# Three scatter accumulators instead of two in an attention and mixture-of-experts block

## The reference, cut to what matters

```
x = x + attention(layernorm(x), ctx)
xn2 = layernorm(x)
scores = softmax(xn2 @ gate_w.T);  topk_w, topk_i = top_k(scores, 4)   # T = 1024 tokens
buf[e]  = tokens of expert e, at most CAP = 128, the rest filled with the spare row T
eout[e] = (silu(xpad[buf[e]] @ w_gate[e]) * (xpad[buf[e]] @ w_up[e])) @ w_down[e] * wbuf[e]
y       = zeros.at[buf].add(eout)[:T]                 # scatter-add over all experts
out     = x + y + silu(xn2 @ sw_gate) * (xn2 @ sw_up) @ sw_down
```

## Time and profile before

| what | value |
| --- | --- |
| median of three timed runs | 219.53 us (214.23, 219.53, 221.49) |
| the profiled execution's own time | 214.88 us |
| its span | 213.1 us, so 1.78 us lie around it |
| PE busy | 185.3 us (87%) |
| DVE busy | 128.1 us (60%) |
| Pool busy | 96.3 us (45%) |
| granted TensorE clock, mean | 0.984 |

### The profile page before, as it was taken

One profiled execution on the slowest core, in us unless ns is written; L12 is line 12 of the kernel. 1 busy time (PEld: TensorE's weight loads), 2 busy tenths in 40 slices (PEclk: granted clock), 3 DMA queues, 4 the chain that ended last, 5 costly groups with the idle time before them and its releaser, 6 DMA issues.

```text
span 213.1 us, 3899 instructions
## 1 busy us (share of the span) xinstructions
PE 185.3 (87%) x1369; PEld 137.5 (65%) x1369; DVE 128.1 (60%) x360; ACT 80.8 (38%) x173; POOL 96.3 (45%) x128
## 2 busy tenths in 40 slices
PE   7884785889798999899968898995999999999980
PEld 2663442767675777568836686783878887676860
DVE  2774696736479845993484546868655553354054
ACT  3583230647355524761296313412123323333000
POOL 7822499862285401530064000034477878867100
PEclk9999999999999999999999999999969999999996
DMA  6789999999559503010861038962044445545865
GB/s 179 203 128 130 132 127 131 126 235 312 179 155 330 136 19 121 3 49 8 240 219 49 3 104 282 310 206 74 28 75 59 78 88 85 82 68 64 213 205 197
DMA packets 22459, 28.94 MB, mean 136 GB/s; under 512 B 2457, under 2 KB 17801, under 8 KB 22441
## 3 DMA queue, kind: packets, MB, share of 16 engines
q1 hardware_dynamic: 18944, 23.06, 45.7%
q0 software_dynamic: 3184, 5.38, 13.2%
q10 hardware_dynamic: 313, 0.27, 0.4%
HBM read 15.91 MB, written 6.42 MB: 105 GB/s over the span
## 4 chain that ended last, share of the span: by engine, by line
PE 40%; DVE 17%; POOL 15%; DMA 13%; issue 9%; ACT 2%; SPq 2%; ACTq 1%; DVEq 0%; POOLq 0%
PE s_ps L1430 7%; DMA odd_d<-y_rows,tok_i 6%; PE m_ps L1446 4%; PE o_ps L1350 4%; DVE top L878 3%; PE m_ps L1388 3%; POOL out L602 3%; PE m_ps L1504 3%; DMA k_rows<-k_parts 2%; DMA xn_t<-odd_d 2%; POOL odd_d L602 2%; PE s_ps L1536 2%; DMA wkv<-in_wkv_t 2%; PE m_ps L1274 2%; PE t_ps L1334 2%
## 5 line engine op out<-in xcount | busy, mean ns | idle before, releaser
L535 POOL TENSOR_SCALAR_AFFINE_SELECT probs<-probs 128x256 f32<-128x256 f32 (+1 forms) x48 | 22.9, 489 | 39.0 <-ACT probs L662 37.8
L878 DVE TENSOR_REDUCE top<-s_ps 128x2 f32<-128x512 f32 (+1 forms) x48 | 32.3, 687 | 7.1 <-PE s_ps L1300 6.4
L662 ACT ACTIVATE probs<-t_ps 128x512 f32<-128x512 f32 x48 | 27.9, 597 | 10.0 <-PE t_ps L1334 6.4
L1430 PE MATMUL s_ps<-xn_t,sgu 128*128 128x256 f32 (+1 forms) x96 | 23.5, 385 | 0.0
L1334 PE MATMUL t_ps<-q_rows,k_rows 128*128 128x256 bf16 (+1 forms) x128 | 19.6, 247 | 1.8 <-ACT probs L662 1.1
L1430 PEld LDWEIGHTS s_ps<-xn_t,sgu 128*128 128x128 f32 (+1 forms) x96 | 16.5, 181 | 3.4 <-issue 0.6
L1297 PE MATMUL s_ps<-mask_b,ident_b 128*128 128x256 bf16 (+1 forms) x48 | 15.0, 312 | 4.2 <-DVE top L878 3.7
L1300 PE MATMUL s_ps<-k_rows,q_rows 128*128 128x128 bf16 (+1 forms) x128 | 18.3, 246 | 0.0
L590 POOL DMA_INDIRECT xn<-xn_d,tok_i x4 | 4.2, 1062 | 25.3 <-DVE tok_i L1053 24.4
L726 ACT ACTIVATE xg_t<-t_ps 128x256 f32<-128x256 f32 x16 | 6.2, 385 | 23.8 <-PE t_ps L1524 23.1
L1334 PEld LDWEIGHTS t_ps<-q_rows,k_rows 128*128 128x128 bf16 x128 | 10.3, 98 | 5.7 <-ACT probs L662 2.6
(11 more groups left out here) (186 smaller groups left out, 390.0 us busy)
## 6 DMA issues: line engine op xcount, KB each, us to landing
k_rows<-k_parts SPq DMA_DIRECT2D x24, 128.0 KB, 6.3
q_rows<-q_parts SPq DMA_DIRECT2D x24, 128.0 KB, 7.5
k_rows<-in_w_dn SPq DMA_DIRECT2D x12, 176.0 KB
out<-xs SPq DMA_DIRECT2D x8, 256.0 KB, 2.4
wgu_early<-in_w_gu SPq DMA_DIRECT2D x4, 352.0 KB
q_rows<-in_w_gu SPq DMA_DIRECT2D x4, 352.0 KB
v_ones<-in_w_gu SPq DMA_DIRECT2D x4, 352.0 KB
probs<-in_w_gu SPq DMA_DIRECT2D x4, 352.0 KB
```

Of the source, the lines that this page charges most:

```text
L535: nc.gpsimd.affine_select(out=v, in_=v, compare_op=ALU.is_ge, fill=0.0, base=0, pattern=[[0, v.shape[1]], [1, P]], channel_multiplier=-1). ...
L662: t_ring.emptied(nc.scalar.activation(probs[:, g % 2, u, :], t_ring.bank(job)[:], ACT.Exp, scale=HD ** -0.5), job)
L878: s_ring.emptied(nc.vector.tensor_reduce(dst, src, AX.X, ALU.max), job)
L1430: last = nc.tensor.matmul(s_ring.bank(("gu", b, c))[0:size, S * half:S * half + S], sgu[:, hc, half, at:at + size], xn2_t[:, hc, S * b:S * ...
```

## The change

Three accumulators in turn: expert e goes to out, second_d or third_d by e modulo 3 (ACCS = 3), so scatter e waits for scatter e-3. third_d is filled with zeros by one more Pool DMA beside the one for second_d (the old odd_d). At the end SP reloads three accumulators instead of two, third_d first, then out, then second_d. The third is loaded into third_rows, which reuses the memory of the first experts' weights, so that a trace prints it as wgu_early. After its last scatter Pool adds third_rows to xs, one batch at a time; DVE waits for Pool's add of that batch and adds second_rows (add_second in place of add_odd).

```diff
+ACCS = 3
-            for n, (acc, dst) in enumerate(((out, xs), (odd_d, odd_rows))):
-                sp.wait_ge(scattered[n], 16 * ((E - LATE) // 2))
+            for n, acc, dst, done in ((2, third_d, third_rows, third_in), (0, out, xs, out_in),
+                                      (1, second_d, second_rows, second_in)):
+                sp.wait_ge(scattered[n], 16 * len(range(n, E - LATE, ACCS)))
...
-                    pool.dma_start(odd_d.rearrange("(t p) c -> p t c", p=P),
-                                   zero_rows[:].unsqueeze(1).to_broadcast([P, (T + CAP) // P, H])).then_inc(zeros_stored, 16)
+                    for acc in (second_d, third_d):
+                        pool.dma_start(acc.rearrange("(t p) c -> p t c", p=P),
+                                       zero_rows[:].unsqueeze(1).to_broadcast([P, (T + CAP) // P, H])).then_inc(zeros_stored, 16)
...
-                if e >= 2:
+                if e >= ACCS:
-                    pool.wait_ge(scattered[e % 2], 16 * (e // 2))
+                    pool.wait_ge(scattered[e % ACCS], 16 * (e // ACCS))
...
+            for b in range(B):
+                pool.wait_ge(third_in[b // 2], 16)
+                pool.wait_ge(out_in[b // 2], 16)
+                v = slice(QT * b, QT * b + QT)
+                nc.gpsimd.tensor_tensor(xs[:, v], xs[:, v], third_rows[:, v], ALU.add).then_inc(third_added, 1)
+                pool.wait_ge(third_added, b + 1)
...
-            def add_odd(b):
+            def add_second(b):
                 v = slice(QT * b, QT * b + QT)
-                dve.wait_ge(sums_in[b // 2], 32)
-                chained(nc.vector.tensor_tensor(xs[:, v], xs[:, v], odd_rows[:, v], ALU.add))
+                dve.wait_ge(third_added, b + 1)
+                dve.wait_ge(second_in[b // 2], 16)
+                chained(nc.vector.tensor_tensor(xs[:, v], xs[:, v], second_rows[:, v], ALU.add))
```

More of the change, by code:

```diff
@@ L183, in build @@
     xn2_d = nc.dram_tensor("xn2_d", [T + CAP, H], F32, kind="Internal").ap()
-    odd_d = nc.dram_tensor("odd_d", [T + CAP, H], F32, kind="Internal").ap()
+    second_d = nc.dram_tensor("second_d", [T + CAP, H], F32, kind="Internal").ap()
+    third_d = nc.dram_tensor("third_d", [T + CAP, H], F32, kind="Internal").ap()
     with ExitStack() as ctx:
@@ L291, in build @@
         spread = reuse(onehot, P, LATE, T)
-        odd_rows = reuse(xn2_t, P, NT, H)
+        second_rows = reuse(xn2_t, P, NT, H)
+        third_rows = reuse(wgu_early, P, NT, H)
         xg_t = sb("xg_t", [P, 2, HC, CAP])
@@ L343, in build @@
         gathered = [sem(f"gathered{e}") for e in range(E)]
-        scattered = [sem(f"scattered{i}") for i in range(2)]
+        scattered = [sem(f"scattered{i}") for i in range(ACCS)]
         spread_ready = sem("spread_ready")
-        sums_in = [sem(f"sums_in{i}") for i in range(2)]
+        out_in = [sem(f"out_in{i}") for i in range(2)]
+        second_in = [sem(f"second_in{i}") for i in range(2)]
+        third_in = [sem(f"third_in{i}") for i in range(2)]
+        third_added = sem("third_added")
         result_ready = sem("result_ready")
@@ L460, in _ @@
             store_base(3)
-            for n, (acc, dst) in enumerate(((out, xs), (odd_d, odd_rows))):
-                sp.wait_ge(scattered[n], 16 * ((E - LATE) // 2))
+            for n, acc, dst, done in ((2, third_d, third_rows, third_in), (0, out, xs, out_in),
+                                      (1, second_d, second_rows, second_in)):
+                sp.wait_ge(scattered[n], 16 * len(range(n, E - LATE, ACCS)))
                 for i in range(2):
                     rows, tiles = slice(T // 2 * i, T // 2 * i + T // 2), slice(NT // 2 * i, NT // 2 * i + NT // 2)
-                    sp.dma_start(dst[:, tiles], acc[rows].rearrange("(t p) c -> p t c", p=P)).then_inc(sums_in[i], 16)
+                    sp.dma_start(dst[:, tiles], acc[rows].rearrange("(t p) c -> p t c", p=P)).then_inc(done[i], 16)
             for b in range(B):
@@ L587, in gather @@
                     pool.wait_ge(xn2_stored[1], 32)
-                    pool.wait_ge(zeros_stored, 48)
+                    pool.wait_ge(zeros_stored, 64)
                 pool.wait_ge(tok_ready, e // 2 + 1)
@@ L598, in scatter @@
                     pool.wait_ge(acc_stored, 16 * B)
-                if e >= 2:
-                    pool.wait_ge(scattered[e % 2], 16 * (e // 2))
+                if e >= ACCS:
+                    pool.wait_ge(scattered[e % ACCS], 16 * (e // ACCS))
                 nc.gpsimd.indirect_dma_start(
-                    out=(odd_d if e % 2 else out)[:, :], out_offset=bass.IndirectOffsetOnAxis(ap=tok_i[:, e:e + 1], axis=0),
+                    out=(out, second_d, third_d)[e % ACCS][:, :], out_offset=bass.IndirectOffsetOnAxis(ap=tok_i[:, e:e + 1], axis=0),
                     in_=y_rows[:, e % Y_BUFS, :], in_offset=None, compute_op=ALU.add,
-                ).then_inc(scattered[e % 2], 16)
+                ).then_inc(scattered[e % ACCS], 16)
             for e in range(2 * SLOTS_AT[0] + 2):
@@ L1086, in expert_out @@
                     n = e - Y_BUFS
-                    dve.wait_ge(scattered[n % 2], 16 * (n // 2 + 1))
+                    dve.wait_ge(scattered[n % ACCS], 16 * (n // ACCS + 1))
                 m_ring.emptied(nc.vector.tensor_scalar(y_rows[:, e % Y_BUFS, :], m_ring.bank(job)[:, 0:H],
@@ L1211, in _ @@
             for b in range(B):
-                add_odd(b)
+                add_second(b)
             dve.wait_ge(dve_chain, n_chain[0])
```

## The result

The changed kernel takes 220.75 us (median of 20 runs), the kernel before 216.36 us (20 runs). The ratio is 1.0212 with a 95% interval of 1.0182 to 1.0242: slower by 2.1%, or 4.6 us by the ratio (4.4 between the medians). The forecast was 220.1 us and +1.7 us; the direction and the range held, the size was short by a factor of nearly three.

The account below looks back on a forecast made before the run. Scatter landings bound the kernel to about 201 us, then reloads and DVE. Waits -1.6, queue +1.1 and adds +2.2 gave +1.7 on a 218.42 mean: 220.1 us (ratio 1.008), range 214.6 to 223.6.

Parts of the forecast that it names:

- Part 1: Scatters at the end: without waits for earlier landings, scatter 13 leaves 1.6 us earlier and second_d is complete at 199.3.
- a new wait for y_rows: Before scatter 13: it can go at 194.57, its rows are there at 194.45, so it just misses this wait.
- Part 2: Reloads at the end: a third megabyte in front leaves 0 to 0.9 us of the 1.6 us gained by earlier scatters.
- the queue is limited by the transfer in front: Reload of odd_d: limited by out's transfer ahead, only partly by scatter 13; its second megabyte needs 2.7 us.
- Parts 3 and 4: Final adds: four Pool adds of 1.24 us from 201.8, taking turns with DVE's; last result 1.7 us later.
- the rival of adds side by side at full speed: Final adds: Pool and DVE do not stall each other; 0.3 us faster to 0.4 slower, about 218.4; chance 0.22.
- Part 5: Extra zero fill before Pool's masks: 1.04 us on Pool, costed at 0; 0.3 without cover, 1.0 at most.
- Part 4: Final adds: DVE instructions with two SBUF inputs stand still during Pool's; eight adds run in a row, ending at 209.2.
- The sum: Whole kernel: -1.6 for waits, 1.1 taken back by the queue, +2.2 for adds waiting on each other: +1.7 us.
- Room between scatters: Gather stage: a third accumulator removes waits at some five scatter pairs in slow executions, giving 215; chance 0.10.
- The fill did not hold Pool: Rival at the zero fills: second fill blocks Pool until the first lands, about 226; chance 0.08, shared with slower scatters.
- The weaker form: End of the kernel: reloads slow scatter 13 by some 2 us, giving 222; within 0.08 shared with the fill holding Pool.

Follow-up runs that it names:

- both repairs: Changed kernel with its zero fills moved to Pool's pause and DVE adding second_rows into PE's sums in PSUM; ratio 1.0131 against the kernel before.

## Why the prediction held, and where its size was off

**Part 1, the waits.** Right in kind, and somewhat high: the forecast had scatter 13 leave 0.6 us after the scaling of its rows begins, 1.6 us sooner than before. It left 0.90 to 0.95 us after it in all eight kernels with three accumulators, so the gain was 1.24 to 1.3 us. The 1.69 us of the pair without out's reload owe 0.44 us to a long wait in the first of them. The forecast that a new wait for y_rows would be just missed was right (0.30 us of issue before each scatter).

**Part 2, the reloads.** This is the step that failed most. The forecast let the queue take back 1.1 of the 1.6 us, had out's first half in at 201.7, 7.7 us after the scaling of expert 13, and second_d's end no later than now, although one more megabyte stood in front. Out's first half came 9.8 us after the scaling, and second_d's second half 13.8 us after it instead of 12.2. In this trace part of it is that third_d's reload was issued 1.4 us later than forecast (scatter 11 left 0.3 us later and landed in 4.98 us instead of 3.83), and 0.6 us that the two pairs took 7.7 us from third_d's issue to out's first half instead of 7.0. But an earlier issue would not have helped, as the kernel with the fills moved and three accumulators shows (rows of DVE, SP and Pool):

```profile
192.92 0.48 DVE L1103 TENSOR_SCALAR y_rows<-m_ps,slot_w 128x256 f32<-128x256 f32 x1 [0.18 <-PE m_ps L1571]
...
193.91 0.93 SPq L474 DMA_DIRECT2D wgu_early<-third_d  x2
...
203.09 5.62 POOL L628 TENSOR_TENSOR xs<-xs,wgu_early 128x512 f32<-128x512 f32 x4 [7.71 <-DMA xs<-out]
```

Third_d's reload is issued 1.0 us after the scaling there, nearly as forecast, and Pool's adds still begin 10.2 us after it. In the kernels with adds in PSUM, adds on DVE and both repairs it is 1.1 us, and the adds begin 9.8 to 10.4 us after the scaling. So the term that was too small is the time of the first two pairs, 7.0 us forecast and 7.7 to 9.3 measured. The remark that the queue is limited by the transfer in front was right and not followed to its end: the run without the third's way back shows the whole gain gone already with two reloads (C 16.19), and the third megabyte then costs 1.33.

**Parts 3 and 4, adds that stand still for each other.** Right, and nearly to the tenth in this trace: from the first add to the last 201.8 to 209.2 = 7.4 us forecast, 206.06 to 213.44 = 7.4 measured. The add took 1.27 us with its inputs in float32 (1.16 was the nearest row). The stretched adds of both engines (DVE 1.78 us, Pool 1.59), which are 0.70 and 1.27 once DVE's input lies in PSUM, rule out the rival of adds side by side at full speed, and the pair with the adds on DVE agrees. Not all of the 2.2 us is standstill; an estimated 0.8 is the wait for Pool.

**Part 5, the second zero fill.** Costed at 0 with 1.0 us "at the very most"; it was 1.0. This step failed, too. The forecast looked only at PE's wait for the masks, 0.3 us, and named DVE's maxima as cover. But DVE itself stood still behind the later masks (1.26 us for an instruction of 0.27) and its maxima came 1.04 us late, by the mechanism that the forecast had in Part 4 and did not apply here; PE was not back in step by 68 us. A is 81.83 to 81.86 us in the seven kernels without an additional fill ahead of the masks and 82.81 to 82.84 in six of the seven with it (in the last, the run without the third's adds, A is 85.99 and its clock fell inside that stretch, so it can't be read). This is the cleanest result of the study.

**The sum.** The forecast had -0.5 + 2.2 = +1.7. Measured by the single steps: +1.0 (fill), +0.1 (waits shortened, gain swallowed), +1.3 (third reload), +2.2 (adds on Pool) = +4.6, close to the timed difference. The last three are differences of C that add up to its 3.66 by construction, so only the timing checks the sum. The trace of one execution can be off by 0.9 us in C: it was 16.94 in the kernel with the fills moved and two accumulators, with nothing in it changed, since its scatter 13 took 6.0 us to land. The forecast gave 0.73 to a result within 2% and 0.13 to slower; the measured 2.1% lies on that line.

**The other rivals.** Room between scatters did not pay widely: with the clock at full speed all through B, it was 51.86 us with three accumulators and 51.64 with two, and no complete kernel with three beat the kernel before. The fill did not hold Pool: two fills were issued in 1.03 and 1.01 us. The weaker form, reloads that slow scatter 13, did come (5.0 to 8.0 us to land against 4.75), but C doesn't follow it: 17.55 us with a landing of 7.3.

**The level of the time.** The three runs of before that the forecast had were spread from 214.23 to 221.49. Over 73 timed runs of that kernel the time falls with the mean granted clock, correlation -0.78, by 1.3 us for each 0.01. That accounts for six tenths of the variance; that the clock is the cause is likely from stretch B and not shown by an edit. The forecast of 220.1 lies so close to 220.75 because its base, 218.4, was 2.0 us above the median of 20 runs while its difference was 2.9 us short: two errors that offset each other.

## What to carry to other kernels

A transfer that was released earlier gained nothing here while another stood in the same queue: before removing a wait ahead of a load, ask when the queue in front of it is empty, and price each added accumulator by its way back (here a megabyte, 1.3 us) and not only by the waits it saves. Work on Pool beside DVE is not free where DVE's inputs lie in SBUF: adds with two inputs there stood still, and so did a small TENSOR_SCALAR with one; with one of an add's inputs in PSUM the same adds ran side by side. So when a change moves Pool's work in time, look at what DVE does at its new place, down to its smallest instruction, and not only at who waits for Pool. Put zero fills and other housekeeping where Pool pauses, even if they take only 1 us.

## What the runs showed that was not expected

An adding scatter lands later beside reloads. Scatter 13, issue to landing: about 3.8 us with no reload's data beside it (four kernels; in one of them out's reload had been issued 1.6 us before the landing), 4.1 to 6.0 beside out's reload (four kernels), 5.0 to 8.0 beside two (six kernels). Plain DMAs with an add to DRAM took 4.5 to 7.6 us and 1.3 to 2.7 us of Pool's time each. The trace before had only one landing beside a reload, 4.75 us, and no plain DMA with an add.

Even the issue of a scatter meets DVE. With DVE's adds in PSUM, the timelines of Pool (scatter 11) and DVE (a one-hot matrix) show:

```profile
193.83 1.89 POOL L612 DMA_INDIRECT third_d<-y_rows,tok_i  x1 [0.30 <-DMA out<-y_rows,tok_i]
...
194.89 0.74 DVE L1112 TENSOR_SCALAR onehot<-rest,tok_f 128x1024 f32<-128x1024 f32 x1
```

A scatter's issue usually takes 1.55 to 1.62 us. This one took 1.89 and ended at 195.72, 0.09 us after DVE's instruction at 195.63. Scatter 11 ends 0.08 or 0.09 us after that instruction in all eight traces with three accumulators, which by these rows is why scatter 13 leaves 0.90 us after the scaling of its rows in most of them and not 0.6. In the kernel before, scatter 10 took 1.68 us and the instruction beside it 1.05 instead of 0.74, so the sign was there. No run tests it.
